# Two graph layers on one core: twelve groups kept on chip in place of eight, rings two and four deep in place of four and eight

## The reference

```
h = relu(layernorm(x))
a = h + scatter_add(dst, relu(h[src] + edge_attr))
z = a @ W1 + b1;  r = relu(batchnorm(z));  y = r @ W2 + b2      # 512 hidden
g = relu(graph norms of y over all nodes)
x1 = x + h + g
h1 = relu(layernorm(x1))
out = x1 + relu(h1 @ W + segment_sum((h1 @ M)[src], dst))
```

## Time and profile before

| what | us |
|---|---|
| median of 3 runs (2696.46 to 2700.9) | 2699.61 |
| the profiled execution | 2695.99 |
| its span in the profile | 2694.3 |
| PE busy | 2460.7 (91%) |
| VectorE busy | 2213.1 (82%) |
| ScalarE busy | 1820.8 (68%) |
| GpSimd busy | 1880.5 (70%) |
| DMA queue of SP | 51.9% of 16 engines' span |
| granted TensorE clock, mean | 0.965 of full |

### The profile page before, as it was taken

The page is one execution under the profiler, slowest core; times in us unless marked ns, Lnnn a source line. Parts: engine busy times, 40 slices in busy tenths (PEclk is TensorE's granted clock), DMA queues, the critical chain, the costliest instruction groups (busy, mean ns, idle before and its releaser), DMA issues. The chain is left out here.

```text
span 2694.3 us, 60001 instructions
## 1 busy us (share of the span) xinstructions
PE 2460.7 (91%) x13809; PEld 2261.5 (84%) x13809; DVE 2213.1 (82%) x6316; ACT 1820.8 (68%) x3905; POOL 1880.5 (70%) x2011
## 2 busy tenths in 40 slices
PE   6787878769999999999999999977999999969997
PEld 4676766649999999999999999976887788858886
DVE  6888788848999999999999999967777777748886
ACT  4777777746666666666666666647988888855554
POOL 5777777758777777777777777717877777737775
PEclk8899999989999999999999999988999999989999
DMA  7987767732444444444444444427999999945663
GB/s 187 212 214 192 211 201 199 196 101 64 141 151 159 145 156 153 150 155 150 151 158 144 157 153 150 154 111 286 398 379 366 372 376 375 379 168 145 169 170 112
DMA packets 312829, 539.70 MB, mean 200 GB/s; under 512 B 74957, under 2 KB 166340, under 8 KB 312759
## 3 DMA queue, kind: packets, MB, share of 16 engines
q1 hardware_dynamic: 252454, 468.18, 51.9%
q0 software_dynamic: 59712, 70.24, 9.6%
q10 hardware_dynamic: 592, 0.54, 0.1%
HBM read 342.53 MB, written 293.34 MB: 236 GB/s over the span
## 5 line engine op out<-in xcount | busy, mean ns | idle before, releaser
L1066 ACT ACTIVATE r<-pair,bnC,bnA 128x384 f32<-128x384 f32 (+1 forms) x524 | 353.8, 675 | 363.2 <-PE pair L1257 361.4
L1021 POOL DMA_INDIRECT ar<-sum_table,idx x391 | 410.9, 1051 | 192.6 <-POOL idx L1017 110.3
L1438 POOL DMA_INDIRECT x1d_table<-x1r,slot x391 | 382.5, 978 | 164.0 <-issue 139.0
L1165 DVE CAST rH<-r 128x384 fp32r<-128x384 f32 (+1 forms) x524 | 437.3, 834 | 52.1 <-ACT r L1066 47.6
L1032 POOL TENSOR_TENSOR xr<-xr,hr 128x768 f32<-128x768 f32 (+1 forms) x123 | 314.9, 2560 | 129.3 <-ACT hr L1051 129.0
L1644 PE MATMUL pair<-Ws,h1T 128*128 128x256 f32 x1564 | 368.5, 385 | 27.3 <-DVE orr L1564 25.4
L835 PE MATMUL bank<-hr 128*128 128x257 f32 (+1 forms) x1564 | 314.5, 357 | 58.3 <-ACT hr L547 58.3
L835 PEld LDWEIGHTS bank<-hr 128*128 128x128 f32 x1564 | 280.4, 211 | 98.4 <-ACT hr L547 63.8
L1273 PE MATMUL bank<-rH,W2h 128*128 128x384 f32 x1048 | 354.5, 338 | 1.7 <-ACT yr L1080 1.7
L1644 PEld LDWEIGHTS pair<-Ws,h1T 128*128 128x128 f32 x1564 | 286.2, 190 | 82.4 <-issue 41.8
L1273 PE MATMUL bank<-rH,W2l 128*128 128x384 f32 x1048 | 354.7, 338 | 0.0
(11 more groups left out here) (217 smaller groups left out, 5665.6 us busy)
## 6 DMA issues: line engine op xcount, KB each, us to landing
xr<-in_x SPq DMA_DIRECT2D x252, 384.0 KB
x_table<-x1r SPq DMA_DIRECT2D x130, 384.0 KB
out<-orr SPq DMA_DIRECT2D x130, 384.0 KB
xh_table<-xr SPq DMA_DIRECT2D x122, 384.0 KB
yT_table<-yr SPq DMA_DIRECT2D x122, 384.0 KB
xhr<-xh_table SPq DMA_DIRECT2D x122, 384.0 KB, 12.0
yr<-yT_table SPq DMA_DIRECT2D x122, 384.0 KB
x1d_table<-blank SPq DMA_DIRECT2D x131, 128.0 KB
```

The source lines that it names most:

```text
L1021: pool.indirect_dma_start(ar[0:p, s, j, :], None, sum_table[:, :], bass.IndirectOffsetOnAxis(ap=idx[0:p, s, j:j + 1], axis=0), bounds_chec ...
L1066: act.activation(r32[:, m, 0:n], z_ps[m][:, 0:n], ACT.Relu, bias=bnC[:, m:m + 1], scale=bnA[:, m:m + 1]).then_inc(r_kept, 1)
L1165: dve.tensor_copy(rH[:, s, m, 0:n], r32[:, m, 0:n]).then_inc(rh_kept, 1)
L1438: pool.indirect_dma_start(x1d_table[:, :], bass.IndirectOffsetOnAxis(ap=slot[0:p, s, j:j + 1], axis=0), x1r[0:p, s, j, :], None, bounds_ch ...
```

## The change

KEPT becomes 12 groups. To make room, in stage 2 the gathered sums ar, the normalized rows hr, the outputs yr and the indices become AU = 2 deep, each with its waits (for the turn, for the addition and xh, for the stored y) on group k-2 in place of k-4; the x rows xr stay four deep. WT moves from hr into r32. NPEEL follows from KEPT and becomes 5. In stage 3 the loads become RL = 4 deep with LEAD = 3; SP's flush grows so that the same last steps run.

```diff
         NU = 4
-        KEPT = 2 * NU
+        AU = 2
+        KEPT = 3 * NU
@@ stage 2, buffers
-            ar = sb("ar2", [P, NU, T, CH], scope=scope)
-            hr = sb("hr2", [P, NU, T, CH], scope=scope)
+            ar = sb("ar2", [P, AU, T, CH], scope=scope)
+            hr = sb("hr2", [P, AU, T, CH], scope=scope)
-            yr = sb("yr", [P, NU, KC, GC], scope=scope)
+            yr = sb("yr", [P, AU, KC, GC], scope=scope)
@@ stage 2, gpsimd
-                        after(pool, t2_made, k - NU + 1)
+                        after(pool, t2_made, k - AU + 1)
@@ stage 2, scalar, norm
-                            after(act, h2_done, k - NU + 1)
-                            after(act, xh2_done, k - NU + 1)
-                        one = act.activation(hr[0:p, s, j, :], xbuf(k, s)[0:p, j, :], ACT.Relu,
+                            after(act, h2_done, k - AU + 1)
+                            after(act, xh2_done, k - AU + 1)
+                        one = act.activation(hr[0:p, h, j, :], xbuf(k, s)[0:p, j, :], ACT.Relu,
@@ stage 2, scalar, keep_y
-                        after(act, yst_done, k - NU + 1)
-                        after(act, y_out[s], 16 * (used - KEPT // NU))
+                        after(act, yst_done, k - AU + 1)
+                        after(act, y_out[s], 16 * (used - KEPT // AU))
@@ stage 3
-        RL = 8
+        RL = 4
         OL = 4
-        LEAD = 6
+        LEAD = 3
...
-                rounds(sp, step, NG - LEAD, RU, 2, LEAD + 8)
+                rounds(sp, step, GROUPS - LEAD, RU, 2, LEAD + 9)
```

More of the change, by code:

```diff
@@ L915, in gnn_kernel @@
         x2_in = [sem(f"x2_in{s}") for s in range(NU)]
-        a2_in = [sem(f"a2_in{s}") for s in range(NU)]
-        y_out = [sem(f"y_out{s}") for s in range(NU)]
+        a2_in = [sem(f"a2_in{s}") for s in range(AU)]
+        y_out = [sem(f"y_out{s}") for s in range(AU)]
         xh_out = [sem(f"xh_out{s}") for s in range(NU)]
@@ L944, in gnn_kernel @@
             r32 = sb("r32", [P, HC, GC], scope=scope)
-            Dm = r32[:, 0:2, :].rearrange("p a b -> p (a b)")[:, 0:512]
-            WT = hr[:].rearrange("p a b c -> p (a b c)")[:, 2 * T * CH:2 * T * CH + KC * HID].rearrange(
+            Dm = r32[:].rearrange("p a b -> p (a b)")[:, 0:2 * CH]
+            WT = r32[:].rearrange("p a b -> p (a b)")[:, 2 * CH:2 * CH + KC * HID].rearrange(
                 "p (a b) -> p a b", a=KC)
@@ L949, in gnn_kernel @@
             rL = sb("rL", [P, 2, HC, GC], FP32R, scope=scope)
-            yr = sb("yr", [P, NU, KC, GC], scope=scope)
+            yr = sb("yr", [P, AU, KC, GC], scope=scope)
             blank = sb("blank", [P, CH], scope=scope)
-            idx = sb("idx2", [P, NU, T], I32, scope=scope)
+            idx = sb("idx2", [P, AU, T], I32, scope=scope)
             def xbuf(k, s):
@@ L986, in step @@
                         k = six[0]
-                        s, _ = ring(six, NU)
+                        s, _ = ring(six, AU)
                         n = columns(k)
@@ L996, in _ @@
                 sp.wait_ge(slots_clear, 16 * NG)
+                for s in range(AU):
+                    sp.wait_ge(y_out[s], 16 * (-(-(NG - s) // AU) - KEPT // AU))
                 for s in range(NU):
-                    stored = -(-(NG - s) // NU) - KEPT // NU
-                    sp.wait_ge(y_out[s], 16 * stored)
-                    sp.wait_ge(xh_out[s], 16 * stored)
+                    sp.wait_ge(xh_out[s], 16 * (-(-(NG - s) // NU) - KEPT // NU))
             @block.gpsimd
@@ L1010, in step @@
                         k = at[0]
-                        s, _ = ring(at, NU)
+                        s, _ = ring(at, AU)
                         p, n = group_shape(k)
-                        after(pool, t2_made, k - NU + 1)
+                        after(pool, t2_made, k - AU + 1)
                         pool.nop(nofuse=True)
@@ L1028, in step @@
                         s, _ = ring(two, NU)
+                        h, _ = ring(two, AU)
                         p, n = group_shape(k)
@@ L1031, in step @@
                         pool.nop(nofuse=True)
-                        pool.tensor_tensor(xbuf(k, s)[0:p, 0:n, :], xbuf(k, s)[0:p, 0:n, :], hr[0:p, s, 0:n, :],
+                        pool.tensor_tensor(xbuf(k, s)[0:p, 0:n, :], xbuf(k, s)[0:p, 0:n, :], hr[0:p, h, 0:n, :],
                                            ALU.add).then_inc(xh2_done, 1)
@@ L1043, in norm @@
                     s, used = ring(at, NU)
+                    h, _ = ring(at, AU)
                     p, n = group_shape(k)
@@ L1072, in keep_y @@
                     k = at[0]
-                    s, used = ring(at, NU)
+                    s, used = ring(at, AU)
                     n = columns(k)
```

## The result

The changed kernel takes **2706.65 us** (median of 8 runs, 2702.33 to 2710.1) against 2696.81 us of the kernel before beside it: ratio 1.0035, 95% interval 1.0023 to 1.0047. The forecast was +2.5 us, its own range up to +9; measured are about +10 by either comparison. The direction is right, most of the amount is something that the forecast does not contain.

The account below looks back on a forecast made before the run. PE bounds stage 2 and both ends of stage 3, the DMA its groups 35 to 126 (slow regime). +0.4 and +2.1 make +2.5 us, on the median 2699.61 giving 2702 us; own range 2696 to 2709, with rivals 2682 to 2724.

Parts of the forecast that it names:

- Stage 2 steady: Stage 2 after its first groups: the two-deep waits have slack, turns stay 9.13 us apart, cost nothing.
- Rival 3: Stage 2: Pool's longer chain or earlier addition makes PE wait, 0.3 us a group, +36 us; chance 0.09.
- Start of stage 2: First groups of stage 2: Pool's memset waits for turn 0, turn 2 comes 0.8 us later; half taken, +0.4 us.
- whose clashes should go: Start of stage 2: Pool, in a fixed place to VectorE sooner, should stop clashing with it; reason for taking half of 0.8.
- Window of four: Stage 3 loads four deep: pace of DMA-bound groups stays 4.42 us; earlier knee and slower last groups cost +2.1 us together.
- the end: Last four groups of stage 3, 127 to 130, lose their load lead: 4.42 us a group instead of 3.99, +1.7 us.
- knee: Stage 3: the point where the slow, DMA-bound pace begins, moving from group 35 to 34, +0.4 us.
- Kept groups: Front of stage 3: 8 fewer transfers save 8.4 us of DMA time, mostly given up as idle time.
- Sum +2.5: Whole kernel: +0.4 us at the start of stage 2 and +2.1 in stage 3, forecast 2702 us.
- Rivals 1 and 2: Stage 3: load window binds, likeliest +19 us, chance 0.20; or shorter queue keeps early rate, -27 us, chance 0.20.

Follow-up runs that it names:

- e7: The change plus 100 tiny memsets ahead of VectorE's stage 4 loop, with stage 3 loads eight deep again, in freed memory: 2677.34 us, ratio 0.9921 to before.
- e2: Kernel before with only the stage 3 loads made four deep (lead of three), eight groups kept: 2703.23 us, ratio 1.0015.
- e3: The change with eight groups kept instead of twelve: 2701.86 us, ratio 1.0014 to the kernel before.
- e5: e3 plus 68 one-element memsets on VectorE ahead of its stage 4 rounds: 2716.45 us, ratio 1.0058 to the kernel before.
- e1: Kernel before with only the stage 2 buffers made two deep, eight groups kept and loads eight deep: 2694.16 us against 2698.37, ratio 0.9992.
- e10: e7 plus an unused tile of 32 bytes per partition behind nmr: 2692.61 us, ratio 0.9984 to the kernel before.
- e4: The changed kernel run once more, nothing altered, for a second profile and median: 2708.18 us, ratio 1.0039 to the kernel before.
- e6: The change plus 100 one-element memsets on VectorE ahead of its stage 4 rounds: 2699.3 us, ratio 1.0004 to the kernel before.
- e9: Kernel before plus one unused tile of 32 bytes per partition behind nmr: 2690.15 us, ratio 0.9983.
- e11: Kernel before plus 32 unused bytes per partition ahead of the weights and 32 more behind nmr: 2693.42 us in one run.
- e8: Kernel before with stage 3 loads only two deep (lead of one): 2798.28 us in one run.

## Why the prediction was right and wrong

- **Stage 2 steady, 0: right.** Turns 9.13 apart with every two-deep kernel but e7 (8.98, the place of the tiles), each engine about where it was put: Pool's chain of gathers takes 5.68 us as forecast, and its xh addition ends 0.6 us before the next turn, 0.7 sooner than the sum had it, since the addition itself became shorter. Rival 3 did not come.
- **Start of stage 2, +0.4: right in size, too simple in kind.** GpSimd's memset waits and turn 2 comes later (12.19 us after turn 0 in place of 11.94). But the larger thing there is rival 3's mechanism, one to three times in every profile of either order: an addition of VectorE that meets one of GpSimd takes 3.05 to 3.16 us in place of 0.96. Timelines of both engines after:

```profile
630.10 3.15 DVE L1132 TENSOR_TENSOR ar<-ar,hr 128x768 f32<-128x768 f32 x1
```

```profile
630.57 1.85 POOL L1034 TENSOR_TENSOR xh_kept<-xh_kept,hr 128x768 f32<-128x768 f32 x1
```

  Turns 0 to 4 take 30.3, 34.3, 35.6, 30.4, 32.7 and 30.7 us in the old order (mean 32.3), 30.5 to 32.1 in seven profiles of the new one at the same pace (mean 31.4). The net cost is none that can be told; the prediction's "whose clashes should go" is half true.
- **Window of four, pace unchanged: slightly wrong.** With eight groups kept, stage 3 takes 557.1 us (mean of e2, e3, e5) in place of 552.8 (before, e1): +4.3. Of it 1.0 is the end, which the prediction had at 1.7 (the last four groups take 17.0 us in place of 16.0, not 17.7). The other 3.5 is a pace that is not quite the same (groups 42 to 126: 4.44 to 4.46 us, 4.41 before), which the step had at nothing. The earlier knee, near group 30, costs nothing that shows: up to group 42 all five take 166.2 to 167.2 us.
- **Kept groups, 8.4 us of DMA time mostly given up: right.** Between 1850 and 1900 us, where PE is busy 50.00 of 50.00, the DMA's share falls from 0.99 to 0.80 (368 to 291 GB/s). Eight-deep loads do not win it back: e10 has 0.81 there. Four more are worth 557.1 - 553.7 = 3.4 us of stage 3 with loads four deep (mean of after, e4, e6), 2.3 with eight (e10). Stage 3 together: +0.9 against +2.1 forecast. The knee came at group 37 or 38, not 34.
- **Sum +2.5: the terms that it has hold together.** Without the gaps the change costs 1.0004 (e6), +1 us, by its interval -2 to +5. In stage 3 the slower pace costs more than forecast, the end costs less and the kept groups give more; that these nearly cancel is luck.
- **Missing term, about 9 us.** The step that failed is the silent one that stage 4 costs nothing since its code is the same. The change writes out one more round of stage 2, VectorE's stage 4 loop moves by 68 or 69 instructions, and each jump back waits 2.4 to 3.6 us for code. Of the 11.2 us of gaps in the first profile only part is lost, since VectorE's waits for gathers shrink from 18.2 to 12.4 us; PE's lower clock after a gap goes with a higher price (294.0 us with two falls, 297.3 and 298.6 with four), though no run separates the two. The page of before could not show the gap, only that the loop is long and that KEPT sets how much code stands ahead of it.
- **Rivals 1 and 2** did not come: the pace was 4.41 between groups 36 and 126, not 4.6 nor 4.13, at 371 to 376 GB/s with windows of either length (2000 to 2200 us).

## What to carry to other kernels

A change that alters how many rounds are written out moves all code behind it; look for idle time before the first instruction of a loop's pass that ends with "issue", and at the packets of the instruction queue, in stages whose source did not change. Judge an edit with one run that moves the code (a few tiny instructions in idle time) and one that moves the tiles (32 unused bytes), or its verdict may be theirs: here about 9 and 15 us against 1 us for the edit itself. Bytes saved at the front of a stage, where another engine sets the pace, are mostly lost as idle time of the DMA: of 8.4 us four more kept groups gave 3.4 with loads four deep and 2.3 with eight.

## What the runs showed of the hardware

- A jump back in VectorE's loop of 311 instructions costs 2.4 to 3.6 us or nothing, by where the loop starts in the program, with 17 to 21 more code packets in 160 us, which hold the four jumps.
- The same fp32r matmuls (128x384) run 8.98, 9.10 or 9.13 us a group with tiles moved by 32 or 64 bytes; the cause is open. Stage 3 was shorter in two of the three kernels so moved (545.5 us in e9, 549.0 in e7, but 550.9 in e11); that is one profile each, e9's from the fastest of its 12 runs, so it may be scatter.
- The DMA moved 371 to 376 GB/s in the slow regime of stage 3, whether loads were four or eight deep (after and before, 2000 to 2200 us), and 328 with two (e8).
- After a gap of PE in stage 4 its granted clock fell to 0.88 over 14 us, in ten gaps of twelve (after, e4, e5); the profiles without gaps have 1.00 there.
- GpSimd's and VectorE's additions hold each other up: 3.15 us for one of VectorE that alone takes 0.96. The Trainium skill, "SBUF — State Buffer", section "Who interferes with whom", says that a VectorE operation with two SBUF inputs contends with a GpSimd one that reads SBUF, and the trace agrees.
